# GpSimd writes a small buffer behind each gather in the first and last pass of every edge sum

## What is computed

```python
def _rgcn_layer(x, W, SW, b, src, dst, rel):
    xt = jnp.einsum('nd,rde->rne', x, W)
    msg = xt[rel, src]
    agg = jax.ops.segment_sum(msg, dst, num_segments=x.shape[0])
    return jax.nn.relu(agg + x @ SW + b)
...
x = _layernorm(x + _rgcn_layer(_rgcn_layer(x, ...), ...))
feat = jax.nn.relu(x @ W1 + b1)
h = feat * d_invsqrt
agg = jax.ops.segment_sum(h[src], dst, num_segments=N)
feat = feat - agg * d_invsqrt
x = _layernorm(x + (feat @ W2 + b2))
```

## Time and profile before

| | |
|---|---|
| median of 3 runs | 7520.16 us (7511.46 to 7523.07) |
| profiled execution | 7492.37 us, its span 7490.5 us |
| TensorE's granted clock, mean | 0.643 of full speed |
| busy: TensorE, VectorE, ScalarE, GpSimd | 45%, 23%, 5%, 63% |
| gathers of sums 1, 2, 3 in the trace | 1661, 1647, 1640, of 0.944 to 0.947 us |

### The profile page before, as it was taken

One profiled execution on the slowest core, in us unless ns is written; L12 is line 12 of the kernel. 1 busy time (PEld: TensorE's weight loads), 2 busy tenths in 40 slices (PEclk: granted clock), 3 DMA queues, 4 the chain that ended last, 5 costly groups with the idle time before them and its releaser, 6 DMA issues.

```text
span 7490.5 us, 50657 instructions
## 1 busy us (share of the span) xinstructions
PE 3400.0 (45%) x13687; PEld 2488.9 (33%) x13841; DVE 1713.6 (23%) x2844; ACT 399.8 (5%) x915; POOL 4709.2 (63%) x4992
## 2 busy tenths in 40 slices
PE   2455455445545454455545544554333333333333
PEld 1333333333333333333333333334333333333333
DVE  3333333333333212222212121221111111111111
ACT  1000000000000000000000000000000000000000
POOL 5666666666666456666666666645666666666665
PEclk7666676666667677767777776775555555555555
DMA  2111111111111111112211211211111111111111
GB/s 57 46 51 49 50 52 50 50 48 51 50 50 53 39 42 54 54 54 57 56 54 55 58 54 56 56 44 44 52 50 51 50 53 51 53 48 52 52 51 48
DMA packets 197581, 382.84 MB, mean 51 GB/s; under 512 B 84323, under 2 KB 93327, under 8 KB 197543
## 3 DMA queue, kind: packets, MB, share of 16 engines
q0 software_dynamic: 159456, 326.88, 16.7%
q1 hardware_dynamic: 36416, 54.67, 2.1%
q10 hardware_dynamic: 1670, 0.85, 0.0%
HBM read 356.43 MB, written 25.65 MB: 51 GB/s over the span
## 4 chain that ended last, share of the span: by engine, by line
another core or an unknown queue 51%; issue 25%; PE 16%; DVE 5%; DVEq 1%; ACT 1%; ACTq 0%; DMA 0%; SPq 0%
PE bank L931 5%; PE bank L961 4%; PE bank L1186 4%; DVE r_S L1023 1%; DVE r_hot L1018 1%; ACT r_agg L885 1%; DVE acc L1062 0%; PE bank L1576 0%; PE bank L945 0%; PE bank L1572 0%; PE bank L1707 0%; DVE d_st L1750 0%; DVEq L1052 0%; DVE d_zr L1762 0%
## 5 line engine op out<-in xcount | busy, mean ns | idle before, releaser
L781 POOL DMA_INDIRECT rows<-in_x_dram,idx x1661 | 1567.6, 944 | 917.3 <-issue 511.9
L781 POOL DMA_INDIRECT rows<-x_d,idx x1647 | 1555.1, 944 | 885.0 <-issue 503.9
L781 POOL DMA_INDIRECT rows<-h_d,idx x1640 | 1552.4, 947 | 825.3 <-issue 790.4
L961 PE MATMUL bank<-r_S,rows 128*128 128x128 f32 x6644 | 1205.3, 346 | 519.5 <-issue 402.4
L1186 PE MATMUL bank<-r_S,rows 128*128 128x64 f32 x3322 | 772.5, 386 | 1425.1 <-issue 1386.9
L961 PEld LDWEIGHTS bank<-r_S,rows 128*128 128x128 f32 x6644 | 1149.5, 258 | 362.3 <-issue 337.5
L1186 PEld LDWEIGHTS bank<-r_S,rows 128*128 128x128 f32 x3322 | 759.4, 317 | 1440.7 <-issue 1440.3
L1023 DVE TENSOR_TENSOR r_S<-bank,key 128x1792 f32<-128x1792 f32 x238 | 480.4, 2019 | 917.3 <-remote 815.8
L885 ACT COPY r_agg<-bank 128x512 f32<-128x512 f32 x476 | 265.8, 586 | 4400.9 <-remote 3081.1
L945 PEld LDWEIGHTS bank<-zeros_bf 128*128 128x128 bf16 x476 | 55.9, 117 | 1267.7 <-ACT r_agg L885 892.3
L1243 DVE TENSOR_TENSOR acc<-acc,bank 128x64 f32 x238 | 52.7, 222 | 1833.1 <-remote 1658.4
(11 more groups left out here) (151 smaller groups left out, 1545.6 us busy)
## 6 DMA issues: line engine op xcount, KB each, us to landing
rows<-in_x_dram,idx POOLq DMA_INDIRECT x1661
rows<-x_d,idx POOLq DMA_INDIRECT x1647
rows<-h_d,idx POOLq DMA_INDIRECT x1640
d_xr<-in_x_dram SPq DMA_DIRECT2D x54, 218.0 KB
x_d<-d_yr SPq DMA_DIRECT2D x27, 218.0 KB
d_x1r<-x_d SPq DMA_DIRECT2D x27, 218.0 KB
h_d<-d_hr SPq DMA_DIRECT2D x27, 218.0 KB
part_d<-d_pr SPq DMA_DIRECT2D x27, 218.0 KB
```

The costliest lines, as they stand in the source:

```text
L781: pool.indirect_dma_start(out=self.c.rows[:, self.place(s), :], out_offset=None, in_=self.table[:, :], in_offset=bass.IndirectOffsetOnAxis ...
L961: mm = pe.matmul(agg_ps[j][:, bass.ds(offs[j * KG + k], TK)], c.rows[:, g.place(h * KG + k), :], S[:, pb, j * KG + k, :], start=False, sto ...
```

## The change

A buffer `c.pause` of 7 tiles (128 x 7 x 128, fp32) is added, which nobody reads. In pass 0 and in the last pass of each sum GpSimd writes a 128x128 part of it with zeros behind every gather. The last such write of a group raises the new semaphore `paused`, and at the head of the next group GpSimd waits for it. There are 56, 42 and 35 such writes in the three first passes and 37 in each last pass. The loop passes and the early gathers stay as they are. After the last pass GpSimd waits once more.

```diff
--- before.py
+++ after.py
@@ -151,6 +151,7 @@
         c.step_t, c.step_g, c.carry = sb("step_t", [P, 1]), sb("step_g", [P, 1]), sb("carry", [P, 1])
+        c.pause = sb("pause", [P, KG, P])
@@ -703,6 +704,7 @@
         self.cleared = sem("cleared")
+        self.paused = sem("paused")
@@ -765,15 +767,21 @@
-        def iteration(q, i, part, set_of, skip=0):
+        def iteration(q, i, part, set_of, skip=0, paused=None):
             at = set_of * UN
             for p in part.pairs:
                 if (p + 1) * PT <= skip:
+                    pool.sem_inc(self.paused, PAIR)
                     continue
                 pool.wait_ge(self.idx_ready, (q * (IT + 1) + i) * PR + p + 1)
                 pool.wait_ge(self.summed, self.pairs_summed(q, i, p))
                 gate(pool, self.c.passed)
                 for h in range(p * PAIR, (p + 1) * PAIR):
+                    if paused is not None and (h + 1) * KG <= skip:
+                        pool.sem_inc(self.paused, 1)
+                    elif paused is not None:
+                        pool.wait_ge(self.paused, paused + (h + 1))
+                        gate(pool, self.c.passed)
                     for k in range(part.of(h)):
                         s, slot = h * KG + k, h if k < halves(part, h) else RING + h % PAIR
                         if s < skip:
@@ -782,17 +790,22 @@
                         ).then_inc(self.landed[slot], 16)
+                        if paused is not None:
+                            ins = pool.memset(self.c.pause[:, k, :], 0.0)
+                    if paused is not None and (h + 1) * KG > skip:
+                        ins.then_inc(self.paused, 1)
 
         def one_round(q, skip=0):
-            iteration(q, 0, FULL, 0, skip)
+            iteration(q, 0, FULL, 0, skip, q * (RING + LEFT.groups))
             with pool.Fori(0, IT // SETS) as n:
                 i = pool.snap(n * SETS)
                 iteration(q, i + 1, FULL, 1)
                 iteration(q, i + 2, FULL, 0)
-            iteration(q, IT, LEFT, 1)
+            iteration(q, IT, LEFT, 1, 0, q * (RING + LEFT.groups) + RING)
 
         self.begin(pool)
         pool.sem_inc(self.cleared, 1)
+        pool.sem_inc(self.paused, 1)
         one_round(0, EARLY[self.turns])
@@ -809,6 +822,8 @@
         pool.end_ifs()
+        pool.wait_ge(self.paused, rounds * (RING + LEFT.groups) + 1)
+        gate(pool, self.c.passed)
         if self.then is not None:
             self.early(pool, rounds, stored)
```

## The result

The changed kernel takes 7422.36 us (median of 4 runs, 7411.14 to 7435.07), the kernel before 7515.81 us (median of 4, 7492.89 to 7523.07). The ratio is 0.9881, with a 95% interval of 0.9853 to 0.991: 93 us less, where 80 were forecast. The profiled execution has a span of 7414.4 us at a granted clock of 0.649, against 7490.5 at 0.643.

A forecast was written before the change was run, and what follows sets the result against it. No engine is full; long gather runs were taken to starve the other engines' issue. First passes -34, -12, -10, last passes -24 and 0 sum to -80 us: 7520 - 80 = 7440, range 7400 to 7600.

The forecast's parts named there:

- the service of the transfers: Behind GpSimd: something serves a gather in about 1.40 us against one issued every 1.25, a debt of 0.15 us each.

The follow-up runs named there:

- even: The changed kernel with writes of 256 bf16 elements and waits only at the head of a pair of groups; 1.0061 of the kernel before, on a kind B chip.

## What to carry to other kernels

A long run of indirect DMAs can go with starved other engines without any semaphore that says so; look for rows of another engine at 2 us and more of idle with no releaser while GpSimd gathers, and compare what they do once it stops. Stops of the issuing engine that grow with the length of the run before them mean that something is slower than it is. Before you call that the service of the transfers, compare when the transfers' packets end and when the engine that uses them starts: here the packets were in time and TensorE was 25 to 47 us late. As long as such stops are there, time added between the gathers comes out of them; where there are none, most of every added tenth of a microsecond is paid. And an addition that is absorbed doesn't say by what: a bound of any kind above the new pace absorbs it. Take the time of the kernel before on more than one chip first: here it decides the sign.

## What the runs showed of the hardware

- A 128x128 fp32 write of GpSimd behind a gather takes 0.22 us and adds 0.09 to the pitch; 128x32 takes 0.15 and adds nothing (1.25 to 1.26 us as without).
- A gather that waits for GpSimd's own write ahead of it starts 0.81 us after that write's end, against 0.17 without the wait.
- The same program, the kernel before, takes 7478 to 7516 us on chips of kind A and 6281 to 6287 on those of kind B; its granted clock is 0.643 to 0.656 and 0.669 to 0.682. The loop passes take 80 to 82 and 70 us.
- On kind A TensorE issues single products about 2 us apart while gathers come at 1.25 us, and starts a group's products 25 to 47 us behind their last packet; with gathers at 1.43 us in the mean this is gone in sum 3 (0.8 us), and less in sums 1 and 2 (35 and 28 us). A gather's last 4096-byte packet starts 2.0 us behind its start (median) in all of them.
- A 128x128 write of GpSimd that starts during a VectorE cast of 1.1 to 1.3 us took 1.05 to 1.17 us instead of 0.22 (0.33 in `even`), in four traces.
